# In each attention slot, a job's values product stands in front of the coming job's scores

## The reference

```python
# magnitude attention (no mask)
sr = (qr @ kr.T + qi @ ki.T) * scale
si = (qi @ kr.T - qr @ ki.T) * scale
scores = jnp.sqrt(sr * sr + si * si)
ctx = softmax(scores) @ v
# causal attention
scores = jnp.where(causal, q @ k.T / sqrt(16), -1e30)
y = softmax(scores) @ v
# then: x + y @ proj_w + proj_b, layer norm, 8 experts, the best two for each token
```

## Time and profile before

| | |
|---|---|
| median of 3 runs | 1024.96 us (1017.67 to 1029.4) |
| the profiled execution | 1020.74 us, its span 1018.8 us |
| granted PE clock, mean | 0.919 |
| PE busy | 897.8 us, 88% of the span |
| DVE, ACT, POOL busy | 648.8, 651.1, 482.7 us |
| chain that ended last | PE 62%, DVE 13%, SP's queue 6%, ACT 6% |

### The profile page before, as it was taken

One profiled execution on the slowest core, in us unless ns is written; L12 is line 12 of the kernel. 1 busy time (PEld: TensorE's weight loads), 2 busy tenths in 40 slices (PEclk: granted clock), 3 DMA queues, 4 the chain that ended last, 5 costly groups with the idle time before them and its releaser, 6 DMA issues.

```text
span 1018.8 us, 21578 instructions
## 1 busy us (share of the span) xinstructions
PE 897.8 (88%) x7037; PEld 699.2 (69%) x7038; DVE 648.8 (64%) x3050; ACT 651.1 (64%) x1386; POOL 482.7 (47%) x509
## 2 busy tenths in 40 slices
PE   3377979989889879999999999467999999999996
PEld 2254556556556456677777776256999999999896
DVE  1666889889788677678877766673344344343341
ACT  2047879788789788988988888264345345344441
POOL 7677656643001101143334333405677677677654
PEclk7567999899899789999999999757999999999999
DMA  7234233231010200010111102426455456565442
GB/s 205 58 72 82 44 67 65 42 64 31 18 32 14 52 1 2 2 38 2 38 39 38 38 2 69 74 55 107 62 110 99 78 109 88 89 108 91 54 51 32
DMA packets 63299, 59.11 MB, mean 58 GB/s; under 512 B 17471, under 2 KB 54242, under 8 KB 63202
## 3 DMA queue, kind: packets, MB, share of 16 engines
q0 software_dynamic: 25344, 27.89, 19.5%
q1 hardware_dynamic: 37666, 29.76, 11.3%
q10 hardware_dynamic: 192, 0.26, 0.1%
HBM read 35.18 MB, written 16.39 MB: 51 GB/s over the span
## 4 chain that ended last, share of the span: by engine, by line
PE 62%; DVE 13%; SPq 6%; ACT 6%; POOL 5%; issue 4%; DMA 2%; POOLq 0%; DVEq 0%; ACTq 0%
PE ps_scores L776 14%; PE ps_ring L768 11%; PE ps_ring L1044 10%; PE ps_ring L776 6%; SPq L500 5%; PE ps_scores L886 5%; PE ps_ctx L903 5%; PE ps_scores L1044 4%; PE ps_scores L889 4%; POOL got L590 3%; DVE probs L1420 2%; ACT probs L1146 1%; DVE probs L1414 1%; ACT square L1137 1%; DMA k<-k_signed 1%
## 5 line engine op out<-in xcount | busy, mean ns | idle before, releaser
L1260 ACT ACTIVATE probs<-ps_scores,fc_bias 128x512 f32<-128x512 f32 (+1 forms) x144 | 88.9, 617 | 171.5 <-PE ps_scores L776 167.6
L650 POOL DMA_INDIRECT out<-z_t,slots_now x80 | 128.1, 1601 | 83.2 <-DVE z_t L1761 58.9
L768 PE MATMUL ps_ring<-ident,probs 128*128 128x128 f32 x768 | 127.2, 291 | 17.2 <-ACT q L1101 8.0
L1128 ACT ACTIVATE prob_t<-ps_ring 128x512 f32<-128x512 f32 x192 | 114.5, 598 | 37.0 <-PE ps_ring L768 36.3
L1137 ACT ACTIVATE square<-ps_scores 128x512 f32<-128x512 f32 x192 | 104.6, 600 | 29.4 <-PE ps_scores L886 24.2
L1153 ACT ACTIVATE probs<-probs,neg_max 128x128 f32<-128x128 f32 x384 | 120.8, 397 | 2.6 <-DVE neg_max L1420 2.6
L768 PEld LDWEIGHTS ps_ring<-ident,probs 128*128 128x128 f32 x768 | 90.5, 147 | 43.4 <-issue 13.0
L1420 DVE CUSTOM_DVE_ANT_0 probs<-ps_scores,causal 128x128 f32<-128x128 f32 x384 | 88.6, 286 | 40.8 <-PE ps_scores L889 40.5
L1044 PE MATMUL ps_ring<-work,probs 128*128 128x192 f32 x672 | 114.5, 326 | 0.0
L1044 PEld LDWEIGHTS ps_ring<-work,probs 128*128 128x128 f32 x672 | 109.3, 190 | 0.1
L1414 DVE CUSTOM_DVE_ANT_0 probs<-square 128x128 f32<-128x128 f32 x384 | 89.2, 287 | 30.6 <-ACT square L1137 30.1
(11 more groups left out here) (230 smaller groups left out, 2056.1 us busy)
## 6 DMA issues: line engine op xcount, KB each, us to landing
k<-k_signed SPq DMA_DIRECT2D x176, 32.0 KB
work<-pj_w SPq DMA_DIRECT2D x8, 576.0 KB, 4.9
token_in<-xin SPq DMA_DIRECT2D x8, 384.0 KB, 3.4
out<-resid SPq DMA_DIRECT2D x8, 384.0 KB, 4.3
vals<-fc_w SPq DMA_DIRECT2D x8, 384.0 KB, 3.5
vals<-fc_w SPq DMA_DIRECT2D x16, 192.0 KB, 4.1
out<-z_t,slots_now POOLq DMA_INDIRECT x80, 3.6
token_in<-xin SPq DMA_DIRECT2D x8, 128.0 KB, 4.3
```

Source lines behind the costliest of these rows:

```text
L650: gp.indirect_dma_start(out[:, :], bass.IndirectOffsetOnAxis(slots_now[:, u, 1, t:t + 1], 0), slot_y[:, o, :], None, compute_op=ALU.add).t ...
L768: return pe.transpose(dst, src, ident[0:n, 0:n])
L1128: sc.activation(prob_t[:, s % 2, :, :], src.rearrange("p (h q) -> p h q", h=4), ACT.Exp if p is mag else ACT.Copy).then_inc(ring_free[i], 1)
L1260: sc.activation(hidden[:, c % 2, f_, 0:128 * nt], ps_scores[:, i, 0:128 * nt], ACT.Gelu, bias=fc_bias[:, e, f_:f_ + 1]).then_inc(gelu_done ...
```

## The change

In PE's `one_pass` the call of `values_product` goes in front of the call of `scores`. Nothing is added or removed; the order of the other four engines is the same as before.

```diff
                     if ready is not None and slot < JOBS:
 
                         fill(*fills.pop(0))
-                    if now is not None and 0 <= slot - SCORE_SLOT[phase_of(now)[0].name] < JOBS:
-                        scores(now, slot - SCORE_SLOT[phase_of(now)[0].name])
                     turned = ready is not None and ready < GROUPS and slot == 1
                     if ready is not None and 1 <= slot <= JOBS and not turned:
                         values_product(ready, slot - 1)
+                    if now is not None and 0 <= slot - SCORE_SLOT[phase_of(now)[0].name] < JOBS:
+                        scores(now, slot - SCORE_SLOT[phase_of(now)[0].name])
                     for n, f in fills:
                         fill(n, f)
```

## The result

The changed kernel takes 1047.99 us (median of 4 runs, 1041.98 to 1051.34), the kernel before 1022.2 us (4 runs): ratio 1.0231, 95% interval 1.0189 to 1.0273, so 25.8 us or 2.3% slower. The forecast was 1045 us in a range of 1026 to 1060. The profiled execution took 1049.51 us, with a span of 1047.5 us, 28.8 us more than the profiled execution before.

The account below looks back on a forecast made before the run. The order of PE's work, 62% of the span in the chain of waits, was taken to bound the kernel. Terms 9.8 + 2.4 + 8.2 = 20.4 us gave 1041.1, by the median (4.2 higher) 1045 us, range 1026 to 1060.

Parts of the forecast that it names:

- The wait at slots 7 and 10: Magnitude passes: values product waits for ScalarE's context copy and holds the scores, net 0.85 us at 11.5 places, 9.8 us.
- The two places counted as covered: Slot 7 of passes 4 and 7: weights' shift or a values projection covers the copy, nothing lost.
- Slot 4: Magnitude passes: key waits hide the copy wait, except in passes 1, 3 and 7, at 0.8 us each: 2.4 us.
- V splitting the key wait: Pass 5: values product splitting the key wait may save one clock drop, 3 us.
- Causal passes: Passes 8 to 14: delays at slots 7, 10 and the pass's end, 1.17 us a pass, 8.2 us together.
- the three terms: In a causal pass: 0.44 us at slot 7, 0.37 at slot 10, 0.36 at the pass's end.
- Pass 15, put at 0: Pass 15: no group follows to be projected and ScalarE sets the pace, so no loss, 0 us.
- The unknown price: Scores directly behind values product, not in the trace before: 0.36 us taken, bounded by -0.1 and +0.1 a slot.
- V did not fill the scores' wait: Rival: values product fills the scores' wait for squares in seven passes, 14 us back, 1011 us; chance 0.08.
- The later waits did not absorb the delay: Rival: waits at pass boundaries, for keys and VectorE take up the delay; some 3 us remain, 1028 us; chance 0.18.
- The clock did not fall behind the new waits: Rival: new waits of 1.18 us in 12 or so places drop PE's clock at 5, 1060 us; chance 0.12.
- The signs: PE's waits: values product waiting for context copy rises from 4 rows to some 30, about 20 us in all.

Follow-up runs that it names:

- second trace of before: The kernel before, unchanged, executed once more for a second trace: 1025.49 us.
- run of the causal ends: Changed kernel with values products behind scores again in slots 4, 7, 10, and in causal passes also slots 3, 11, 12: 1027.56 us, ratio 1.0035 against the kernel before.
- Second trace after: The changed kernel, not altered further, executed once more for a second trace: 1048.24 us.
- the first experiment: The changed kernel with the values product behind the scores again in slots 4, 7 and 10 only: 1034.49 us, ratio 1.011 against the kernel before.
- the mirror run: The kernel before with the values product ahead of the scores in slots 4, 7 and 10 alone: 1039.83 us, ratio 1.016.
- 8.4 alone: The kernel before with values products in front only in passes that score a causal group: 1033.35 us, ratio 1.012.

## Why the prediction was right, and where it was not

**The wait at slots 7 and 10 (9.8 us).** Right in mechanism and size. Predicted: 1.18 us idle, then 0.36 for V, the next S at 0.71, and "about 6.6" between the scores of jobs 4 and 7. Measured in pass 6: 1.12, 0.36, 0.71, 6.62. Over passes 1 to 7, the distances between the copies of slots 6, 9 and 12 grew against the second trace of before by 9.1 us in sum in the first trace and 9.7 in the second. In clean passes (2, 5 and 6) slot 7 gave 0.92 and slot 10 0.84. The two places counted as covered, slot 7 of passes 4 and 7, gave between -0.06 and 0.01.

**Slot 4 (2.4 us).** Right in size where nothing disturbs the place; what the traces show beyond it is not slot 4's wait. The distance from the copy of slot 3 to that of slot 6 grew by these amounts (first trace, second trace):

| pass | 1 | 2 | 3 | 4 | 5 | 6 | 7 | sum |
|---|---|---|---|---|---|---|---|---|
| first | 3.6 | 2.3 | 0.8 | -0.1 | -2.0 | -0.3 | 0.5 | 4.8 |
| second | 0.9 | 2.7 | 0.8 | 0.4 | -2.0 | -0.6 | 2.5 | 4.7 |
| forecast | 0.8 | 0 | 0.8 | 0 | 0 | 0 | 0.8 | 2.4 |

In passes 1 and 3 the place costs 0.8 to 0.9, the value taken, at a granted clock of 1.00; the reason given, "they run at half clock there", does not hold at this slot in pass 3, where its S takes 0.71 before and after. The two large values, 3.6 in pass 1 of the first trace and 2.5 in pass 7 of the second, are stretches at a lower clock. Pass 1 of the first and then of the second trace, and pass 7 of the second:

```profile
108.06:117.37 9.31, 6.97 (x63) 3.85 (x63) 7.49 (x42) 5.23 (x12) 5.44 (x6) 0.74 0.08 23
```

```profile
106.18:112.81 6.63, 5.50 (x63) 3.31 (x63) 6.53 (x39) 5.23 (x12) 3.08 (x5) 1.00 0.11 17
...
361.41:371.41 10.00, 9.15 (x75) 5.94 (x76) 5.55 (x36) 6.54 (x13) 3.05 (x6) 0.75 0.06 16
```

The run of the causal ends, with V behind in slot 4, shows much the same in pass 7, 9.68 us at a clock of 0.75, where the traces of before have 8.04 at 0.90 and 7.51 at 0.97.

In pass 2 the key wait was as long as the prediction says, in the first trace of before:

```profile
146.81 0.71 PE L886 MATMUL ps_scores<-k,q 32*128 32x256 f32 x8 [1.13 <-DMA k<-k_signed]
```

Both traces after show something else there: ScalarE idles ahead of the squares, and the copy stands behind both. Second trace after, ScalarE, then PE:

```profile
151.79 1.08 ACT L1137 ACTIVATE square<-ps_scores 128x512 f32<-128x512 f32 x2 [2.52 <-remote]
...
153.24 0.51 ACT L1160 ACTIVATE ctx_t<-ps_ctx 128x384 f32<-128x384 f32 x1
```

```profile
153.89 0.65 PE L903 MATMUL ps_ctx<-prob_t,work 128*32 128x128 f32 x8 [3.62 <-ACT ctx_t L1160]
154.47 1.24 PE L886 MATMUL ps_scores<-k,q 32*128 32x256 f32 x8
```

That looks like a price of the new order, but the first experiment, with V behind in slot 4, has the same idle time (2.43 us) ahead of the same squares, and there S waits for them:

```profile
152.79 1.62 PE L886 MATMUL ps_scores<-k,q 32*128 32x256 f32 x8 [2.41 <-ACT square L1139]
```

Its growth in pass 2 is 2.2 us, beside 2.3 and 2.7 in the changed kernel. So most of it is ScalarE's idle time at this place, which stops PE in either order; in the second trace of before the idle time (2.41 us) fell ahead of a copy of P instead. Taken against the first experiment, V in front in slot 4 costs 0.1 and 0.5 us in pass 2.

Passes 4 and 6 are hidden as forecast. Pass 5 gains 2.0, since the slow stretch behind its key wait is gone (mean granted clock there 0.81 in the second trace of before, 1.00 in both after). In the second trace of before that wait was 1.70 us, and the next scores took 1.23; in the changed kernel V's wait of 0.77 stands in its place, and the scores behind it keep their usual 0.71 and 1.06:

```profile
270.88 0.71 PE L886 MATMUL ps_scores<-k,q 32*128 32x256 f32 x8 [1.70 <-DMA k<-k_signed]
...
272.93 1.23 PE L886 MATMUL ps_scores<-k,q 32*128 32x256 f32 x8
```

```profile
281.95 0.43 PE L903 MATMUL ps_ctx<-prob_t,vals 128*32 128x128 f32 x8 [0.77 <-ACT ctx_t L1160]
282.30 0.71 PE L886 MATMUL ps_scores<-k,q 32*128 32x256 f32 x8
...
283.89 1.06 PE L886 MATMUL ps_scores<-k,q 32*128 32x256 f32 x8
```

The prediction named that possibility, V splitting the key wait, and did not count it. V in slot 4 is neither needed for it nor enough: the run with slots 4, 7 and 10 behind gains 2.1 in pass 5, with a key wait of 1.05 us at this place and 0.71 for the next scores, and the mirror run, with V in front in these slots alone, gains nothing there (9.66 us at a clock of 0.72, where the two traces of before have 10.20 and 8.96).

**Causal passes (8.2 us).** Right (9.2 and 7.7 in the table above, 8.4 alone), but for pass 15. Pass 11, the answer to the earlier trace rows, PE and ScalarE:

```profile
511.98 0.42 PE L903 MATMUL ps_ctx<-prob_t,vals 128*32 128x128 f32 x8 [0.56 <-ACT ctx_t L1160]
512.34 0.50 PE L889 MATMUL ps_scores<-k,q 32*128 32x128 f32 x8
...
518.90 0.43 PE L903 MATMUL ps_ctx<-prob_t,vals 128*32 128x128 f32 x8 [0.30 <-ACT ctx_t L1160]
519.26 0.50 PE L889 MATMUL ps_scores<-k,q 32*128 32x128 f32 x8
```

```profile
511.36 0.48 ACT L1160 ACTIVATE ctx_t<-ps_ctx 128x384 f32<-128x384 f32 x1
...
518.28 0.48 ACT L1160 ACTIVATE ctx_t<-ps_ctx 128x384 f32<-128x384 f32 x1
```

V starts 0.14 behind the copies' ends (511.84 and 518.76), with S behind it. From the first profiled execution before to that after, the scores of pass 9 shift by 22.14 us up to slot 6, 22.58 in slots 8 and 9, 22.95 in slots 10 to 12, and the first of pass 10 by 23.31: 0.44, 0.37 and 0.36, the three terms. Pass by pass the shift grows by 1.15 to 1.17 in passes 9 to 12, and by 1.08 and 0.82 in passes 13 and 14. The tail's reason, VectorE getting the scores late, is what the run of the causal ends supports. Pass 15, put at 0, cost 0.9 in both traces after (from its first context copy to that of pass 16): V waits there for the copy, 0.94 us in slot 7 and 0.21 in slot 10. The trace before hinted at it: of the 4 rows in which V waits for the copy, which the prediction puts into pass 16, one of 0.26 us stands in slot 7 of pass 15.

**The unknown price.** V to S is 0.36 (327.80 to 328.16, 511.98 to 512.34), the value taken. By the Trainium skill, "TensorEngine Tiling (Array Packing)", Key Properties, a change of mode drains TensorE, which by the prediction's count of changes costs as much in either order. The trace agrees as far as the prices go: V to P was 0.35 and S to V 0.65 there, and S to P is 0.64 now (325.38 to 326.02).

**The rivals.** V did not fill the scores' wait: with the copy out of the way, at 309.15, S is stretched to 1.06 as before. The later waits did not absorb the delay. The clock did not fall behind the new waits of 1.12 us: after both of pass 6 the scores take 0.71, the duration of the 2.4 GHz level, and over the magnitude passes the mean granted clock was 0.94, beside 0.95 before. The Trainium skill, "TensorE: Matmul & The Clock Gate", Part 1, has idleness throttle TensorE. The trace agrees for the key waits of 1.52 and 1.70 us and for V's 3.62 in pass 2, behind which the scores take 1.23 to 1.24, not for these waits of 1.12, nor for a key wait of 1.69 in pass 4 of the first experiment, behind which the scores keep 0.71.

**The signs.** V's wait was to rise to "some 30" rows and "about 20 us"; it rose to 38 and 33.8. Slots 7 and 10 of the magnitude passes hold 14.9 us in 12 places, beside 11.5 x 1.18 = 13.6 by the forecast. The excess lies mostly in slot 4, with 9.9 us in 7 places: 0.77 each in passes 4 to 6, where it stands in for the key wait, and 4.7 in pass 2.

**The sum.** The mechanism is the forecast's. Its size was short: 20.4 us were forecast; the medians gave 25.8, the second traces of both kernels 22.8, the first 28.8. Of the 5.4 us by which the medians exceed it, pass 15 accounts for 0.9. The other 4.5 are no larger than what two executions of the kernel before differ by, 4.6 us, nearly all of it in the magnitude passes: stretches at the lower clock, and idle time of ScalarE whose cause is open. That 1045 came within 3 us of 1048 is partly luck: it took the median of before at 4.2 us above the profiled execution, and with a fourth run that median is 1.5 above.

## What to carry to other kernels

When an instruction is moved ahead in an engine's queue, ask which wait it brings along, and where the engine that releases it does that work in its own queue. Here 26 us hung on a half-microsecond copy that stood behind work for the very instruction it now held up; moving the copy as well took them away, and moving it alone cost some 6. Before a growth seen at one place is charged to the change, look at the same place in a run that has the old order there: in pass 2 that run shows almost all of it.

## What the runs showed that was not expected

- ScalarE idles for 1.0 to 4.8 us at one or two places in passes 1 and 2, at other instructions from kernel to kernel, in ten of the twelve traces here, without a releaser that the profile shows ("remote"); the first trace of the kernel before had none. The cause stays open.
- Two executions of the same kernel differed by 4.6 us at pass 16 (the kernel before) and by 1.9 (the changed one), all of it made before pass 9; from pass 9 to pass 14 they ran apart by 0.06 us or less.
